# One attention-and-experts kernel: the second block's rows are loaded ahead of the keys and the third's behind them, and TensorE's first pass for the maximum and the turned maximum move ahead of pieces of the keys

## The chip, the cores and the metric

The kernel runs on one NeuronCore of one Trainium2 chip. The metric is the device time of one execution in microseconds (us). The kernel before takes 274.97 us, the median of three runs (274.79 to 275.19). In what follows PE is TensorE (PEld its weight loads), DVE is VectorE, ACT is ScalarE, POOL is GpSimd and SP is SyncE, which here only issues DMAs.

## The reference

1024 tokens of 128 values attend to 6404 keys of 96 values, and then go through a mixture of 8 experts, two of which are used for each token.

```python
def layernorm(x): return (x - mean(x)) / sqrt(var(x) + 1e-5)

def attention(xn, ctx):
    q, k, v = xn @ Wq + bq, ctx @ Wk + bk, ctx @ Wv + bv
    return softmax(q @ k.T / sqrt(128)) @ v

def ffn(xn):
    route = softmax(xn @ Wr + br)
    routed = top-2 of route, scaled to sum 1
    h = relu(xn @ W1[e] + b1[e])
    return sum over e of routed[e] * (h @ W2[e] + b2[e])

x = x + tanh(g_xattn) * attention(layernorm(x), ctx)
x = x + tanh(g_ffn)   * ffn(layernorm(x))
```

## The kernel before, in words

**Tiling.** The 8 tiles of 128 tokens form three blocks of 2, 3 and 3 tiles (`BLOCK_TILES`). The keys form 51 chunks of 128, of which the last holds 4 keys. Loads come in groups of 8 chunks (`NATURAL_GROUP`), transposes in windows of 4 chunks (`WINDOW`, 13 windows, 0 to 12), and the attention of one block goes through 26 units of 2 chunks.

**Precision.** A float32 product is made of three fast products: each operand is split into a rounded part (`_hi`) and the rest (`_lo`). The scores of a chunk are `ctxT_hi*q_hi + ctxT_hi*q_lo + ctxT_lo*q_hi` (L1473 to L1475).

**The softmax's shift.** The maximum of a row is estimated first from the hi parts alone: `score_for_max(s)` on PE makes one *slot*, the scores of one tile of tokens against up to 1024 keys (L1395, two matmuls of 512), and `reduce_max(s)` on DVE reduces it (L999). The first block needs, before its first unit, only round 0: six slots, the two tiles against keys 0 to 1023 (slots 0 and 1, windows 0 and 1), 1024 to 2047 (slots 2 and 3) and 2048 to 3071 (slots 4 and 5). `finish_max(0)` on DVE joins them into `nmax` (L1006), `turn_max(0)` on PE turns `nmax` into a row (L1408), `row_max(0)` on DVE adds it to row 96 of `q_hi` (L1014), and then the product itself subtracts the maximum. Slot s waits until slot s-2 has been reduced, and slot 1 also waits for `q_lo`.

**The start**, the place of this change. There is no scheduler: every engine's instructions stand in the order in which the code writes them, and semaphores tie the engines together.

- SP (L503 to L524) issues the first block's rows of x (`tok`, semaphore `x_in`), the two parts of Wk, group 0 of the keys (8 chunks, 384 KB), all other rows of x (6 tiles, 384 KB, `x_later_in`), groups 1 to 6 of the keys, and then the small constants.
- DVE: `statistics(0, 0)` and the normalized rows of the first block (L1032); then it waits for `x_later_in`, takes `statistics(0, 1)` and `statistics(0, 2)` of the second and third block (L981, L984, L986), makes `q_lo` (L991), the six reductions, `finish_max(0)`, `row_max(0)`, and splits windows 9, 10 and 11 (L1021).
- PE: 10, 4 and 6 warm-up transposes (L1335; the 6 are `WARM_NORM`) around the folding of the weights, the first block's rows turned (`turn_x(0, 0)`, L1368), windows 0 and 1 (`turn_window`, L1359, one transpose for each chunk), the folded q of the block (`make_qk(0)`, L1375), windows 2 and 3, then the six slots with two windows behind slots 1, 3 and window 8 last, the second block's rows, windows 9 and 10, `turn_max(0)`, windows 11 and 12, and then the units: `scores` and, two units later, `values` (L1499 to L1501).
- ACT copies each turned window twice, rounded (`ctxT_hi`, L799) and, for windows 0 to 8, whole (`ctxT_f`, L804); `q_hi` (L814) stands behind the rounded copies of windows 0 and 1. Each unit then takes two exponentials on ACT (L906, L910) and one subtraction on DVE (L1214, `ex_lo`); the scores of unit u wait for `ex_lo` of unit u-2.
- POOL makes `rstd` of each block (L609), the normalized rows of the second and third block (L616), and the `_lo` parts of windows 0 to 8 (L638) and of the keys (L645, L647).

The functions in full:

Of the kernel before, what the change touches and what calls it, by code (L numbers as in the profile page):

```python
# [35 lines left out]
BLOCK_TILES = [2, 3, 3]  # L36
# [3 lines left out]
WINDOW = 4  # L40
# [4 lines left out]
W_RING = 2  # L45
WARM_UP = 10
WARM_FOLD = 4
WARM_NORM = 6
EPS = 1e-5


# [36 lines left out]
def attention_experts(nc, x, ctx, g_xattn, g_ffn, wq, bq, wk, bk, wv, bv, w1, b1, w2, b2, wr, br, out):  # L88
# [83 lines left out]
    with ExitStack() as stack:  # L172
# [3 lines left out]
        def sem(name):  # L176
            return stack.enter_context(nc.semaphore(name))
# [143 lines left out]

        small_in, x_in, w_consts_in = sem("small_in"), sem("x_in"), sem("w_consts_in")
        x_later_in = sem("x_later_in")
        ctx_in = [sem(f"ctx_in{g}") for g in range(NG)]
        w_in = [sem(f"w_in{r}") for r in range(W_SLOTS)]
        out_done = sem("out_done")
# [45 lines left out]
        def tiles(b):  # L372
            return slice(FIRST_TILE[b], FIRST_TILE[b] + BLOCK_TILES[b])
# [130 lines left out]
        def _(sync):  # L504
            sync.dma_start(tok[:, tiles(0), :], xv[:, tiles(0), :]).then_inc(x_in, 16)
            sync.dma_start(wk_sb[0:C, :], wk).then_inc(small_in, 16)
            sync.dma_start(wk_sb[C:CA, :], bk.rearrange("(a h) -> a h", a=1)).then_inc(small_in, 16)
            for g in range(NG):
                js = group_chunks(g)
                whole = min(js[-1] + 1, FULL)  # L510
                sync.dma_start(raw[:, js[0]:whole, :], ctxv[:, js[0]:whole, :]).then_inc(ctx_in[g], 16)
                if g == 0:
                    later = slice(BLOCK_TILES[0], NT)
                    sync.dma_start(tok[:, later, :], xv[:, later, :]).then_inc(x_later_in, 16)
            sync.wait_ge(pad_zeroed, 1)
            sync.dma_start(raw[0:TAIL, FULL, :], ctx[0, FULL * P:NKEY, :]).then_inc(ctx_in[NG - 1], 16)
            sync.dma_start(wv_sb[0:C, 0:HID], wv).then_inc(w_consts_in, 16)
# [72 lines left out]
        def _(pool):  # L590
# [50 lines left out]
            def split_ctx(g):  # L641
                js = group_chunks(g)
                hi = ch[:, js[0]:js[-1] + 1, 0:C]
                pool.wait_ge(ctx_in[g], 16 if js[-1] < FULL else 32)
                nc.gpsimd.tensor_copy(hi, raw[:, js[0]:js[-1] + 1, :]).then_inc(ctx_hi_ready, 1)  # L645
                pool.wait_ge(ctx_hi_ready, g + 1)
                nc.gpsimd.tensor_tensor(cl[:, js[0]:js[-1] + 1, :], raw[:, js[0]:js[-1] + 1, :],  # L647
                                        hi.bitcast(F32), ALU.subtract).then_inc(ctx_lo_ready, 1)
# [321 lines left out]
        def _(dve):  # L970
# [8 lines left out]
            def statistics(which, b):  # L979
                for t in range(BLOCK_TILES[b]):  # L980
                    last = nc.vector.bn_stats(stats[:, which, FIRST_TILE[b] + t, :], tok[:, FIRST_TILE[b] + t, :])  # L981
                step(last)
                for t in range(BLOCK_TILES[b]):
                    last = nc.vector.bn_aggr(mv[:, which, FIRST_TILE[b] + t, :], stats[:, which, FIRST_TILE[b] + t, :])  # L984
                step(last)
                nc.vector.tensor_scalar(veps[:, which, tiles(b)], mv[:, which, tiles(b), 1], EPS, None,  # L986
                                        ALU.add).then_inc(var_ready, 1)
# [14 lines left out]
            def finish_max(r):  # L1002

                ts = tiles(ROUND_BLOCK[r])
                dve.wait_ge(max_reduced, SLOTS_UNTIL[r])
                nc.vector.tensor_reduce(nmax[:, ts], pmax[:, ts, ROUND_AT[r]:ROUND_AT[r] + PLACES[r] + (1 if r == 1 else 0)], AX.X, ALU.max,  # L1006
                                        negate=True).then_inc(nmax_ready, 1)
# [26 lines left out]
            last.then_inc(first_norm, 1)  # L1034
            dve.wait_ge(x_later_in, 16)
            statistics(0, 1)
            statistics(0, 2)
            split_q(0)
            for s in range(SLOTS_UNTIL[0]):
                reduce_max(s)  # L1040
            finish_max(0)
            row_max(0)
            for w in range(TURNED_BY_VECTOR, NW - 1):
                split_window(w)
# [286 lines left out]
        def _(pe):  # L1331
# [15 lines left out]
            def turn_window(w):  # L1347

                js = window_chunks(w)
                pe.wait_ge(ctx_in[js[0] // NATURAL_GROUP], 16 if js[-1] < FULL else 32)  # L1350
                if 4 <= w < TURNED_BY_VECTOR:
                    pe.wait_ge(ctxT_f_ready, w - 3)
                elif w >= TURNED_BY_VECTOR + 2:

                    pe.wait_ge(max_reduced, SLOTS_UNTIL[0] - (NW - 1 - w))
                elif w >= TURNED_BY_VECTOR:
                    pe.wait_ge(ctxT_f_ready, w - 2)
                for k, j in enumerate(js):
                    last = nc.tensor.transpose(window_bank(w)[0:C, k * P:(k + 1) * P], raw[:, j, :], ident[:, :])  # L1359
                last.then_inc(ctx_turned, 1)  # L1360
# [52 lines left out]
            turn_window(0)  # L1413
            turn_window(1)
            make_qk(0)
            for w in range(2, 4):
                turn_window(w)
            for s in range(SLOTS_UNTIL[0]):
                score_for_max(s)
                w = 4 + s  # L1420
                if s % 2 and w < TURNED_BY_VECTOR:
                    turn_window(w - 1)
                    turn_window(w)
            turn_window(TURNED_BY_VECTOR - 1)
            pe.wait_ge(ctxT_f_ready, TURNED_BY_VECTOR - 3)
            turn_x(0, 1, x_home(1))
            for w in range(TURNED_BY_VECTOR, NW - 2):
                turn_window(w)
            turn_max(0)
            for w in range(NW - 2, NW):  # L1430
                turn_window(w)

            def beside_first_block(i):
# [300 lines left out]
```

## Time and profile before

| | us |
|---|---|
| median of 3 runs | 274.97 (274.79 to 275.19) |
| the profiled execution's own time | 274.55 |
| its span in the trace | 272.8 |
| PE busy in the span | 266.0 (98%) |
| DVE, ACT, POOL busy | 210.5, 186.8, 109.3 |
| mean granted TensorE clock | 0.999 of full |

The page lists the share of the span in which each engine had an instruction under way. Its chain of waits is followed back from the last instruction, at each step to what released it. The timeline gives start, duration and the instruction; where a row ends in `xN`, N instructions are merged, and a bracket says how long the engine had been idle and which event ended that. Line numbers are those of the kernel before unless said otherwise.

### The profile page before, as it was taken

To read this page: it belongs to the slowest core of one execution; us is meant where nothing else is said; L and a number is where in the kernel's file an instruction comes from. 1 tells how busy PE (TensorE), PEld (TensorE's weight loads), DVE (VectorE), ACT (ScalarE), POOL (GpSimd) and SP (SyncE) were. 2 spreads that over 40 slices of the span, in tenths; PEclk is the share of its full clock that TensorE was granted. 3 is DMA by queue.
4 is the path that set the end of the run, shared out by engine and by line. 5 is a ranking of instruction groups with operands and counts; after the bars stand their busy time and mean duration, and the time that the engine had idled before them with its cause. 6 is when DMAs were issued, how large, how long until landed. Compare 5 with 4: busy or idle time off the path is not lost.

```text
span 272.8 us, 5070 instructions
## 1 busy us (share of the span) xinstructions
PE 266.0 (98%) x1662; PEld 245.4 (90%) x1662; DVE 210.5 (77%) x406; ACT 186.8 (69%) x338; POOL 109.3 (40%) x144
## 2 busy tenths in 40 slices
PE   7999999999999999999999999999999999999994
PEld 7677989999999999999889999999889998999993
DVE  4889977897486898789637478876688699467696
ACT  2997575445675556556577798888546664999990
POOL 3899993556800030000001553661025444355720
PEclk9999999999999999999999999999999999999999
DMA  6700020000099100000000222435301011313312
GB/s 191 275 2 0 0 82 0 2 1 2 0 248 338 42 0 2 0 1 2 1 0 2 77 77 79 117 126 145 106 15 37 24 32 35 91 58 73 86 53 81
DMA packets 18485, 17.08 MB, mean 63 GB/s; under 512 B 2410, under 2 KB 14940, under 8 KB 18460
## 3 DMA queue, kind: packets, MB, share of 16 engines
q1 hardware_dynamic: 17372, 15.31, 18.7%
q0 software_dynamic: 640, 1.31, 1.7%
q8 instruction: 14, 0.23, 0.3%
q10 hardware_dynamic: 448, 0.14, 0.2%
q14 instruction: 11, 0.09, 0.1%
HBM read 13.34 MB, written 3.42 MB: 61 GB/s over the span
## 4 chain that ended last, share of the span: by engine, by line
PE 87%; DVE 8%; DMA 2%; issue 1%; ACT 1%; SPq 1%; DVEq 0%
PE ps L1473 9%; PE ps L1499 9%; PE ps L1474 9%; PE ps L1500 9%; PE ps L1501 9%; PE ps L1475 9%; PE ps L1395 7%; PE ps L1600 4%; PE ps L1586 3%; DVE pmax L999 2%; DMA tok<-in_x_dram 2%; PE ps L1575 2%; PE ps L1625 2%; PE ps L1627 2%; PE ps L1626 2%; PE ps L1601 2%
## 5 line engine op out<-in xcount | busy, mean ns | idle before, releaser
L906 ACT ACTIVATE ex_hi<-ps 128x768 fp32r<-128x768 f32 (+1 forms) x78 | 56.9, 730 | 55.9 <-PE ps L1475 54.4
L1214 DVE TENSOR_TENSOR ex_lo<-ps,ex_hi 128x768 fp32r<-128x768 f32 (+1 forms) x66 | 58.4, 885 | 23.0 <-ACT ps L910 20.7
L999 DVE TENSOR_REDUCE pmax<-ps 128x1 f32<-128x512 f32 (+2 forms) x74 | 62.4, 874 | 10.3 <-PE ps L1395 9.5
L1499 PE MATMUL ps<-ex_hi,ctx_both 128*97 128x384 f32 (+1 forms) x153 | 49.7, 325 | 0.0
L910 ACT ACTIVATE ps<-ps 128x768 f32<-128x768 f32 (+1 forms) x66 | 49.7, 752 | 0.0
L1474 PE MATMUL ps<-q_lo,ctxT_hi 96*128 96x384 f32 (+1 forms) x153 | 49.0, 321 | 0.0
L1475 PE MATMUL ps<-q_hi,ctxT_lo 96*128 96x384 f32 (+1 forms) x153 | 48.6, 318 | 0.0
L1500 PE MATMUL ps<-ex_hi,ctx_both 128*96 128x384 f32 (+1 forms) x153 | 48.6, 318 | 0.0
L1501 PE MATMUL ps<-ex_lo,ctx_both 128*97 128x384 f32 (+1 forms) x153 | 48.6, 318 | 0.0
L1473 PE MATMUL ps<-q_hi,ctxT_hi 97*128 97x384 f32 (+1 forms) x126 | 42.3, 336 | 0.3 <-DVE ex_lo L1214 0.2
L1395 PE MATMUL ps<-ctxT_hi,q_hi 97*128 97x512 f32 (+1 forms) x104 | 34.3, 400 | 0.7 <-DVE pmax L999 0.4
L609 POOL TENSOR_TENSOR rstd<-veps,minus_half 128x3 f32<-128x3 f32 (+1 forms) x6 | 5.0, 829 | 74.6 <-DVE veps L986 74.4
L1474 PEld LDWEIGHTS ps<-q_lo,ctxT_hi 96*128 96x128 f32 x153 | 29.1, 190 | 0.3
L1475 PEld LDWEIGHTS ps<-q_hi,ctxT_lo 96*128 96x128 f32 x153 | 29.1, 190 | 0.0
L1500 PEld LDWEIGHTS ps<-ex_hi,ctx_both 128*96 128x96 f32 x153 | 24.8, 162 | 3.3
L1499 PEld LDWEIGHTS ps<-ex_hi,ctx_both 128*97 128x97 f32 x153 | 24.8, 162 | 2.8 <-issue 0.7
L1501 PEld LDWEIGHTS ps<-ex_lo,ctx_both 128*97 128x97 f32 x153 | 24.8, 162 | 1.4
L1473 PEld LDWEIGHTS ps<-q_hi,ctxT_hi 97*128 97x128 f32 x126 | 23.7, 188 | 2.5 <-issue 1.1
L1307 DVE TENSOR_TENSOR ex_lo<-ps,ex_hi 128x384 fp32r<-128x384 f32 x32 | 17.7, 554 | 9.3 <-ACT ps L948 8.0
L742 POOL TENSOR_TENSOR shared<-shared 128x128 f32<-128x128 f32 x17 | 8.2, 485 | 31.8 <-ACT shared L937 31.6
L669 POOL TENSOR_TENSOR ex_lo<-shared,ex_hi 128x512 fp32r<-128x512 f32 (+1 forms) x12 | 14.8, 1239 | 13.3 <-PE ps L1501 11.5
L1395 PEld LDWEIGHTS ps<-ctxT_hi,q_hi 97*128 97x128 f32 x104 | 17.4, 189 | 2.5 <-DVE pmax L999 1.2
(227 smaller groups left out, 545.2 us busy)
## 6 DMA issues: line engine op xcount, KB each, us to landing
raw<-in_ctx_dram SPq DMA_DIRECT2D x6, 384.0 KB, 6.1
w_raw<-in_L_ffn_W_dram SPq DMA_DIRECT2D x8, 256.0 KB, 3.9
raw<-in_L_ffn_W_dram SPq DMA_DIRECT2D x8, 256.0 KB, 6.3
raw<-in_L_ffn_b_dram SPq DMA_DIRECT2D x8, 256.0 KB
shared<-routing SPq DMA_DIRECT2D x8, 192.0 KB
x_slots<-shared SPq DMA_DIRECT2D x1, 1088.0 KB, 6.3
y_slots<-shared SPq DMA_DIRECT2D x17, 64.0 KB, 1.5
shared<-in_L_ffn_b_dram SPq DMA_DIRECT2D x1, 512.0 KB, 3.4
```

Source lines behind the costliest of these rows:

```text
L906: nc.scalar.activation(ex_pair(ex_hi, u % P_RING, js, n), scores, ACT.Exp)
L910: nc.scalar.activation(whole, scores, ACT.Exp).then_inc(ex_ready, 1)
L999: nc.vector.tensor_reduce(pmax[:, FIRST_TILE[ROUND_BLOCK[r]] + t, place:place + 1], max_home(s)[:, 0:w], AX.X, ALU.max).then_inc(max_reduc ...
L1214: nc.vector.tensor_tensor(ex_pair(ex_lo, u % P_RING, js, n), whole, ex_pair(ex_hi, u % P_RING, js, n).bitcast(F32), ALU.subtract).then_inc ...
L1307: nc.vector.tensor_tensor(hid(ex_lo, u), bank_of_hidden(u)[:, 0:SPAN], hid(ex_hi, u).bitcast(F32), ALU.subtract).then_inc(h_lo_ready, 1)
L1395: last = nc.tensor.matmul(max_home(s)[:, at:at + n], q_hi[:, ft * P:(ft + 1) * P], ctxT_hi[0:CA, key + at:key + at + n], start=True, stop= ...
L1473: nc.tensor.matmul(dst, ctxT_hi[0:CA, keys], q, start=True, stop=False)
L1474: nc.tensor.matmul(dst, ctxT_hi[0:C, keys], q_lo[:, span(b)], start=False, stop=False)
L1475: last = nc.tensor.matmul(dst, ctxT_lo[0:C, keys], q_hi[0:C, span(b)], start=False, stop=True)
L1499: nc.tensor.matmul(dst[0:CA, :], ch[:, j, :], hi, start=(j == first), stop=False)
L1500: nc.tensor.matmul(dst[0:C, :], cl[:, j, :], hi, start=False, stop=False)
L1501: last = nc.tensor.matmul(dst[0:CA, :], ch[:, j, :], lo, start=False, stop=(j == final))
```

## The change

On SP, the second block's rows (3 tiles, 192 KB, `x_later_in`) are issued ahead of the keys; group 0 of the keys is issued as two halves of 4 chunks with a semaphore each (`ctx_first_in` for window 0); the third block's rows (192 KB, `x_last_in`) are issued behind the last group. On DVE, `statistics(0, 2)` moves from ahead of `q_lo` to between `finish_max(0)` and `row_max(0)`, behind a wait for `x_last_in`. On PE, `WARM_NORM` falls from 6 to 2, windows 2 and 3 move from ahead of slot 0 to behind it, and windows 9 and 10 move behind `turn_max(0)`. POOL's `split_ctx(0)` waits for both halves. No computation is added or taken away but the four warm-up transposes; there is one DMA more in group 0 and one more for x.

```diff
-WARM_NORM = 6
+WARM_NORM = 2
...
+            sync.dma_start(tok[:, tiles(1), :], xv[:, tiles(1), :]).then_inc(x_later_in, 16)
             for g in range(NG):
                 js = group_chunks(g)
                 whole = min(js[-1] + 1, FULL)
+                if g == 0:
+                    sync.dma_start(raw[:, 0:WINDOW, :], ctxv[:, 0:WINDOW, :]).then_inc(ctx_first_in, 16)
+                    js = js[WINDOW:]
                 sync.dma_start(raw[:, js[0]:whole, :], ctxv[:, js[0]:whole, :]).then_inc(ctx_in[g], 16)
-                if g == 0:
-                    later = slice(BLOCK_TILES[0], NT)
-                    sync.dma_start(tok[:, later, :], xv[:, later, :]).then_inc(x_later_in, 16)
+            sync.dma_start(tok[:, tiles(2), :], xv[:, tiles(2), :]).then_inc(x_last_in, 16)
...
             dve.wait_ge(x_later_in, 16)
             statistics(0, 1)
-            statistics(0, 2)
             split_q(0)
             for s in range(SLOTS_UNTIL[0]):
                 reduce_max(s)
             finish_max(0)
+
+            dve.wait_ge(x_last_in, 16)
+            statistics(0, 2)
             row_max(0)
...
             def turn_window(w):
                 js = window_chunks(w)
-                pe.wait_ge(ctx_in[js[0] // NATURAL_GROUP], 16 if js[-1] < FULL else 32)
+                if w == 0:
+                    pe.wait_ge(ctx_first_in, 16)
+                else:
+                    pe.wait_ge(ctx_in[js[0] // NATURAL_GROUP], 16 if js[-1] < FULL else 32)
...
             make_qk(0)
-            for w in range(2, 4):
-                turn_window(w)
+
             for s in range(SLOTS_UNTIL[0]):
                 score_for_max(s)
-                w = 4 + s
-                if s % 2 and w < TURNED_BY_VECTOR:
+                w = 3 if s == 0 else 4 + s
+                if (s == 0 or s % 2) and w < TURNED_BY_VECTOR:
                     turn_window(w - 1)
                     turn_window(w)
             turn_window(TURNED_BY_VECTOR - 1)
             pe.wait_ge(ctxT_f_ready, TURNED_BY_VECTOR - 3)
             turn_x(0, 1, x_home(1))
-            for w in range(TURNED_BY_VECTOR, NW - 2):
-                turn_window(w)
             turn_max(0)
-            for w in range(NW - 2, NW):
+            for w in range(TURNED_BY_VECTOR, NW):
                 turn_window(w)
```

How the instructions stand, first on PE at the start. L1335 is a warm-up transpose, L1368 turns rows of x, L1359 turns a chunk of keys, L1375 makes q, L1395 is half a slot. Before:

```order
L1335 MATMUL ps<-ident 128x128 x6
L1368 MATMUL ps<-ident,norm 128x128 x2
L1359 MATMUL ps<-ident,raw 96x128 x8
L1375 MATMUL ps<-xT,mq_sb 97x256
L1359 MATMUL ps<-ident,raw 96x128 x8
L1395 MATMUL ps<-ctxT_hi,q_hi 128x512 x4
L1359 MATMUL ps<-ident,raw 96x128 x8
L1395 MATMUL ps<-ctxT_hi,q_hi 128x512 x4
```

And in the changed kernel, where the same lines are L1345, L1381, L1372, L1388 and L1408:

```order
L1345 MATMUL ps<-ident 128x128 x2
L1381 MATMUL ps<-ident,norm 128x128 x2
L1372 MATMUL ps<-ident,raw 96x128 x8
L1388 MATMUL ps<-xT,mq_sb 97x256
L1408 MATMUL ps<-ctxT_hi,q_hi 128x512 x2
L1372 MATMUL ps<-ident,raw 96x128 x8
L1408 MATMUL ps<-ctxT_hi,q_hi 128x512 x2
L1372 MATMUL ps<-ident,raw 96x128 x8
L1408 MATMUL ps<-ctxT_hi,q_hi 128x512 x4
```

Slot 0 now stands ahead of windows 2 and 3, and slot 1 between them and windows 4 and 5.

PE at the end of round 0, from the last two slots to the first unit. L1408 turns the maximum and L1473 is the first matmul of unit 0. Before:

```order
L1395 MATMUL ps<-ctxT_hi,q_hi 128x512 x4
L1359 MATMUL ps<-ident,raw 96x128 x4
L1368 MATMUL ps<-ident,norm 128x128 x3
L1359 MATMUL ps<-ident,raw 96x128 x8
L1408 MATMUL ps<-ident,nmax 1x128 x2
L1359 MATMUL ps<-ident,raw 96x128 x7
L1473 MATMUL ps<-q_hi,ctxT_hi 128x256
```

In the changed kernel (L1421 turns the maximum, L1483 begins unit 0):

```order
L1408 MATMUL ps<-ctxT_hi,q_hi 128x512 x4
L1372 MATMUL ps<-ident,raw 96x128 x4
L1381 MATMUL ps<-ident,norm 128x128 x3
L1421 MATMUL ps<-ident,nmax 1x128 x2
L1372 MATMUL ps<-ident,raw 96x128 x15
L1483 MATMUL ps<-q_hi,ctxT_hi 128x256
```

Eight transposes went from ahead of the turned maximum to behind it, where there are now 15 instead of 7.

DVE, from the first block's normalized rows to the split windows. Before:

```order
L1032 TENSOR_SCALAR norm<-tok,mv,rstd 128x128 x2
L981 BN_STATS stats<-tok 128x6 x3
L984 BN_AGGR mv<-stats 128x2 x3
L986 TENSOR_SCALAR veps<-mv 128x3
L981 BN_STATS stats<-tok 128x6 x3
L984 BN_AGGR mv<-stats 128x2 x3
L986 TENSOR_SCALAR veps<-mv 128x3
L991 SCALAR_TENSOR_TENSOR q_lo<-ps,bias_col,q_hi 96x256
L999 TENSOR_REDUCE pmax<-ps 128x1 x6
L1006 TENSOR_REDUCE nmax<-pmax 128x2
L1014 TENSOR_TENSOR q_hi<-ps,q_hi 1x256
L1021 TENSOR_TENSOR ctxT_lo<-ps,ctxT_hi 96x512 x3
```

In the changed kernel:

```order
L1040 TENSOR_SCALAR norm<-tok,mv,rstd 128x128 x2
L989 BN_STATS stats<-tok 128x6 x3
L992 BN_AGGR mv<-stats 128x2 x3
L994 TENSOR_SCALAR veps<-mv 128x3
L999 SCALAR_TENSOR_TENSOR q_lo<-ps,bias_col,q_hi 96x256
L1007 TENSOR_REDUCE pmax<-ps 128x1 x6
L1014 TENSOR_REDUCE nmax<-pmax 128x2
L989 BN_STATS stats<-tok 128x6 x3
L992 BN_AGGR mv<-stats 128x2 x3
L994 TENSOR_SCALAR veps<-mv 128x3
L1022 TENSOR_TENSOR q_hi<-ps,q_hi 1x256
L1029 TENSOR_TENSOR ctxT_lo<-ps,ctxT_hi 96x512 x3
```

The third block's seven instructions of statistics left the place ahead of `q_lo` and stand between `nmax` and the row of the maximum.

## Rows read from the trace of the kernel before

**Rows 1.** The page: granted TensorE clock in 40 slices; the chain's shares by engine.

```profile
PEclk9999999999999999999999999999999999999999
...
PE 87%; DVE 8%; DMA 2%; issue 1%; ACT 1%; SPq 1%; DVEq 0%
```

**Rows 2.** Chain of waits, first 25 us: start us, us, what.

```profile
7.37 0.69 DVE stats L981 x3
...
8.60 0.59 DVE stats L981 x3
...
10.11 6.80 DVE pmax L999 x6
16.93 0.17 DVE nmax L1006
...
17.15 0.60 PE ps L1408 x4
...
19.41 0.60 ACT ex_hi L906
```

**Rows 3.** DMA issues in windows 2.03:2.4, 2.4:2.9, 2.9:3.4: KB each, us to landing.

```profile
raw<-in_ctx_dram SPq DMA_DIRECT2D x1, 384.0 KB, 4.3
...
tok<-in_x_dram SPq DMA_DIRECT2D x1, 384.0 KB, 4.9
...
raw<-in_ctx_dram SPq DMA_DIRECT2D x1, 384.0 KB, 5.4
```

**Rows 4.** Timeline of SP's queue: the issues of those three.

```profile
2.06 0.35 SPq L511 DMA_DIRECT2D raw<-in_ctx_dram  x1
2.45 0.43 SPq L514 DMA_DIRECT2D tok<-in_x_dram  x1
2.93 3.46 SPq L511 DMA_DIRECT2D raw<-in_ctx_dram  x6
```

**Rows 5.** Timeline of PE: start us, us, instruction, [idle before <-releaser].

```profile
5.79 0.86 PE L1335 MATMUL ps<-ident 128*128 128x128 f32 x6
...
6.71 1.04 PE L1359 MATMUL ps<-ident,raw 128*96 128x128 f32 x8
...
9.17 0.71 PE L1395 MATMUL ps<-ctxT_hi,q_hi 97*128 97x512 f32 x2
10.17 0.73 PE L1395 MATMUL ps<-ctxT_hi,q_hi 97*128 97x512 f32 x2 [0.29 <-DVE q_lo L991]
10.74 1.04 PE L1359 MATMUL ps<-ident,raw 128*96 128x128 f32 x8
11.53 0.71 PE L1395 MATMUL ps<-ctxT_hi,q_hi 97*128 97x512 f32 x2
...
15.27 0.60 PE L1359 MATMUL ps<-ident,raw 128*96 128x128 f32 x4
...
16.04 1.04 PE L1359 MATMUL ps<-ident,raw 128*96 128x128 f32 x8
...
17.68 0.97 PE L1359 MATMUL ps<-ident,raw 128*96 128x128 f32 x7
18.41 0.36 PE L1473 MATMUL ps<-q_hi,ctxT_hi 97*128 97x256 f32 x1
```

**Rows 6.** Timeline of ACT.

```profile
7.34 1.07 ACT L799 CAST ctxT_hi<-ps 97x512 fp32r<-97x512 f32 x2
8.30 0.49 ACT L814 ACTIVATE q_hi<-ps,bias_col 97x256 fp32r<-97x256 f32 x1
...
17.24 2.08 ACT L799 CAST ctxT_hi<-ps 96x512 fp32r<-96x512 f32 x4
```

**Rows 7.** Timeline of DVE.

```profile
5.23 0.60 DVE L1032 TENSOR_SCALAR norm<-tok,mv,rstd 128x128 f32<-128x128 f32 x2 [0.92 <-POOL rstd L609]
...
17.78 0.43 DVE L1014 TENSOR_TENSOR q_hi<-ps,q_hi 1x256 fp32r<-1x256 f32 x1 [0.69 <-PE ps L1408]
```

**Rows 8.** Timeline of POOL: the lo parts of windows 0 to 3.

```profile
12.06 4.97 POOL L638 TENSOR_TENSOR ctxT_lo<-w_raw,ctxT_hi 96x512 fp32r<-96x512 f32 x4
```

More of the change, by code:

```diff
@@ L323, in attention_experts @@
         x_later_in = sem("x_later_in")
+        ctx_first_in = sem("ctx_first_in")
+        x_last_in = sem("x_last_in")
         ctx_in = [sem(f"ctx_in{g}") for g in range(NG)]
@@ L643, in split_ctx @@
                 hi = ch[:, js[0]:js[-1] + 1, 0:C]
+                if g == 0:
+                    pool.wait_ge(ctx_first_in, 16)
                 pool.wait_ge(ctx_in[g], 16 if js[-1] < FULL else 32)
```

## The prediction

> **What bounds the kernel now.** I read the page first. The chain that ended last lies for 87% on PE and for 8% on DVE [rows 1], so nearly everything behind the start is PE's own work. The change leaves that work as it is. It can only move the time at which the first unit starts, so I read the first 25 us of the chain of waits. There the limit is DVE: it waits for the later rows of x, takes two sets of statistics from 7.37, and then runs six reductions back to back from 10.11 to 16.93, 1.14 us each; nmax follows, PE turns it at 17.15, and the first exponential starts at 19.41 [rows 2]. Of everything in the change I therefore ask what it does to three times: when slot 0 reaches DVE, when nmax is taken (N, 16.93 now), and when the first exponential starts (X, 19.41 now). From X on the same instructions follow in the same order, so a shift of X should be a shift of the end.
>
> **The loads.** Group 0 of the keys is issued at 2.06, the rows of x at 2.45, group 1 at 2.93 [rows 4], and they land 4.3, 4.9 and 5.4 us later [rows 3]: at 6.36, 7.35 and 8.33. That is 384 KB every 0.98 us, in order of issue, so I take bytes in order as the rule: 192 KB cost 0.49 us. The new order puts the second block's rows at 6.36 - 0.49 = 5.87, window 0's half at 6.36, window 1's at 6.85 and group 1 at 7.84. So window 0's keys come when all of group 0 came before, and what follows is half a microsecond earlier until the third block's rows, which come last.
>
> The Trainium skill (DMA: Bandwidth & Descriptors, Anatomy of one DMA) gives a DMA about 2.0 us plus its bytes at 436 GB/s, for the path through GpSimd. By that page's figures, as an estimate, 192 KB issued at 2.45 land at 4.9, and the keys would not be waited for at all. The trace disagrees for this queue: 384 KB took 4.3 to 5.4 us here [rows 3], since each DMA stands behind the ones ahead of it. I go by the trace.
>
> **Slot 0.** Before, windows 0 and 1 start on PE at 6.71, behind the warm-up and the turned rows [rows 5]. ACT begins to copy window 0 at 7.34 (0.63 later), copies two windows in 0.96 and makes q_hi from 8.30 to 8.79 [rows 6]. Slot 0 could then have started near 8.85, but two other things held the reductions: windows 2 and 3 stood ahead of it on PE, to 9.17 [rows 5], and q_lo stood behind the statistics on DVE, so that slot 0, ready at 9.17 + 0.71 = 9.88, was reduced from 10.11 [rows 2, 5]. After the change the normalized rows are ready at 5.83 as before [rows 7]. Four warm-up transposes less (0.86 for 6, overlapping [rows 5], so about 0.5) let PE turn them at once, which would allow window 0 from about 6.2. It then waits for its keys to 6.36, and window 1 for its half to 6.85. Window 1 sets the rest: its copy begins 0.63 later, q_hi another 0.48 later and takes 0.49, and 0.06 passes to PE. Slot 0 starts at t = 6.85 + 0.03 + 0.63 + 0.48 + 0.49 + 0.06 = **8.54**. Its scores reach DVE at t + 0.76 = 9.30. The second block's statistics (1.23 from set to set [rows 2]) are over by 7.2, and q_lo (0.4) fits between q_hi and slot 0. So the first reduction starts 0.81 earlier than now.
>
> **A new gap.** Half of that is given back. A slot holds PE for 0.57 (10.17 to 10.74), two windows for 0.79 (10.74 to 11.53) [rows 5]. The new order has windows 2 and 3 behind slot 0 and windows 4 and 5 behind slot 1, so slot 2 starts at t + 2 x (0.57 + 0.79) = t + 2.72 and its scores are there at t + 3.48, while DVE has finished two reductions at t + 0.76 + 2.27 = t + 3.03. DVE idles 0.45. Slots 3 to 5 stay ahead of DVE. N = t + 0.76 + 6.82 + 0.45 = t + 8.03 = **16.57**, 0.36 earlier than 16.93.
>
> **Behind nmax.** Before, windows 9 and 10 ran from 16.04, in the time in which PE had to wait for nmax anyway [rows 5]; they cost nothing there. Now they come after it. PE turns the maximum 0.22 after N, starts the windows 0.53 later (17.15 to 17.68), and 7 transposes take 0.73 to the first unit at 18.41 [rows 2, 5], 0.104 each. Fifteen take 1.56, which is 0.83 more. The first unit starts at 16.57 + 0.22 + 0.53 + 1.56 = **18.88** in place of 18.41, and X follows 1.00 later as now, at 19.88.
>
> Is another engine later than that? ACT: window 9's copy can begin only at 17.32 + 0.63 = 17.95. Three more starts at 0.48 and the last copy (0.49) end at 19.88, at the same moment; before, ACT had begun these four at 17.24 and was through at 19.32 [rows 6]. DVE: third-block statistics from 16.74 take 1.23, and row_max, now behind them, runs 17.97 to 18.40 instead of 17.78 to 18.21 [rows 7]. PE reaches the first unit 0.48 after that, so the statistics cost nothing as long as the 15 transposes cover them. If windows 9 and 10 were still ahead, the row would be the limit, at about 18.45. What is queued behind the new wait for the third block's rows is row_max and then the split windows; those rows land near 13, over 3 us ahead. POOL: its split of windows 0 to 3 ends at 17.03 [rows 8], and the second block's normalized rows, which stand ahead of it, come no later than now. SP's two more issues and POOL's longer wait for group 0 lie behind landed loads with microseconds to spare. I cost these at nothing.
>
> **Sum.** -0.36 (N earlier) + 0.83 (windows behind it) = +0.47, rounded to **+0.5** because two engines meet at X. The profiled execution took 274.55, of which the span is 272.8, so its twin would take 275.05; the median of before is 0.42 above that execution, so I put the changed kernel's median at **275.5**. What a measurement of this kernel can tell from no change is about 0.2%, 0.55 us, and the sum lies just inside.
>
> **The bounds.** The unknown is the landing of the two halves with shorter runs. Below, PE is held only by the turned rows: t = 8.35 and X +0.3. Above, if DMAs cost by number and not by bytes, window 1's half lands third, at 8.33: t = 10.0 and X +1.9. I stay near the lower one, since the rows show bytes in order at a steady pace.
>
> **Rivals.**
>
> *The keys come late (slower).* If halves with half the run length move more slowly, window 1's half lands after 7.1 instead of 6.85. For it: the load stands behind 192 KB of x that PE does not need. Against: the steady 0.98 us steps. From a delay of 0.25 on, the sum is +0.7; with half of the upper bound it is +1.2, 276.2. Chance 0.18.
>
> *The clock falls (slower).* All 40 slices show the granted clock at 0.9 or more of full, the 2.4 GHz level [rows 1]. After slot 5 PE would now turn window 8 and the second block's rows, then idle from 15.7 to 16.8 where before it turned windows, then turn 15 chunks. If the clock fell to 1.2 GHz there, those 15 transposes and unit 0 (1.56 + 1.00) would take up to twice as long: +2.6 on top, 278.1. The Trainium skill (TensorE: Matmul & The Clock Gate, Part 4: PE-mode transpose) says that transposes do not count as busy for the clock as matmuls do, and by that rule this stretch, with fewer warm-ups ahead, is a risk. The trace disagrees so far: from 15.27 to 18.41 PE did little but transposes already, and the clock held. Chance 0.05.
>
> *The shift is absorbed (no change).* DVE paces units 2 to 4, so a late X might be made up there. Against it: DVE's work there starts from X's own result, and nothing in it is taken out. It would give 275.0 to 275.2. Chance 0.17.
>
> *The end is earlier (faster).* N would have to come 1.4 us earlier, to pay 0.83 for the windows and 0.55 more: slot 0 at t = 7.5 at the latest. That needs q_hi by 7.4, when window 0's keys have landed for 1 us and two copies stand ahead on ACT. I see no way but a gain in later units that the trace does not announce. 274.3. Chance 0.09.
>
> **Numbers.** The forecast itself has 0.51, for X from +0.3 to +0.75; six tenths of that fall within 0.2%. Same: 0.6 x 0.51 + 0.15 of the absorbed case = 0.46. Slower: 0.4 x 0.51 + 0.18 + 0.05 + the other 0.02 of it = 0.45. Faster: 0.09. The range goes from 274.7 (some absorption, and run-to-run spread of 0.2) to 276.3 (the late keys with half the bound), and leaves out the faster case and the clock.
>
> **What would show it.** Right: slot 0 near 8.5; a gap of about 0.4 on DVE between the second and third reduction; nmax near 16.6; PE idle about a microsecond ahead of the turned maximum; 15 transposes behind it and the first unit near 18.9; row_max done before that; X near 19.9 and no difference later. Wrong: window 0 or 1 waiting for its keys past 7.0, nmax later than 16.9 or earlier than 16.2, the first unit waiting for row_max, a granted clock below full between 16 and 20, or a gain or loss behind 25 us.

## The result, and the profile after

The changed kernel takes 275.81 us, the median of seven runs (275.78 to 276.18), against 274.97 (274.61 to 275.20) for the kernel before, timed beside it: slower by 0.84 us, ratio 1.0034 with a 95% interval of 1.0022 to 1.0046. The forecast was 275.5 in a range of 274.7 to 276.3, with nearly even chances for "the same" and "slower". In the runs below two executions lie more than 1.5% above the fastest of their kernel, at 279.35 with the addition on POOL and at 279.21 for the kernel before in the third set; the ratios leave them out, and without them those two medians are 275.94 and 275.20.

| us | before | worked out | after |
|---|---|---|---|
| profiled execution (its span) | 274.55 (272.8) | 275.05 | 275.78 (274.0) |
| slot 0 starts on PE | 9.17 | 8.54 | 8.42 |
| first reduction starts | 10.03 (10.11 in [rows 2]) | 9.30 | 9.17 |
| nmax is taken (N) | 16.93 | 16.57 | 16.49 |
| first unit starts on PE | 18.41 | 18.88 | 19.57 |
| first exponential starts (X) | 19.41 | 19.88 | 20.59 |

Up to N everything came as worked out, to within 0.13. From X on, the shift of 1.18 is carried to the end, where it is 1.23; in the chains of waits the same instructions stand 1.15 later near 70 us and 1.22 near 200. The time was lost between N and the first unit, and more of it than forecast.

First the loads. These are the DMA issues in four short stretches, with KB each and us to landing, for the issues at 2.06, 2.46, 2.93 and 3.4:

```profile
tok<-in_x_dram SPq DMA_DIRECT2D x1, 192.0 KB, 3.4
...
raw<-in_ctx_dram SPq DMA_DIRECT2D x1, 192.0 KB, 3.6
...
raw<-in_ctx_dram SPq DMA_DIRECT2D x2, 192.0 KB, 3.6
...
raw<-in_ctx_dram SPq DMA_DIRECT2D x1, 384.0 KB, 4.2
```

They land at 5.5, 6.1, 6.5 and 7.6, each 0.2 to 0.4 earlier than worked out from [rows 3]. PE's timeline, which answers to [rows 5]:

```profile
8.42 0.71 PE L1408 MATMUL ps<-ctxT_hi,q_hi 97*128 97x512 f32 x2 [0.75 <-ACT q_hi L822]
8.96 1.04 PE L1372 MATMUL ps<-ident,raw 128*96 128x128 f32 x8
9.76 0.71 PE L1408 MATMUL ps<-ctxT_hi,q_hi 97*128 97x512 f32 x2
10.31 1.04 PE L1372 MATMUL ps<-ident,raw 128*96 128x128 f32 x8
11.10 1.42 PE L1408 MATMUL ps<-ctxT_hi,q_hi 97*128 97x512 f32 x4
...
16.70 0.60 PE L1421 MATMUL ps<-ident,nmax 128*1 128x128 f32 x4 [0.96 <-DVE nmax L1014]
17.23 1.84 PE L1372 MATMUL ps<-ident,raw 128*96 128x128 f32 x15
19.57 0.39 PE L1483 MATMUL ps<-q_hi,ctxT_hi 97*128 97x256 f32 x1 [0.49 <-DVE q_hi L1022]
```

Ahead of slot 0 PE waits for q_hi, and the trace shows no wait for keys before it. Slot 2 starts 2.68 after slot 0 (2.72 worked out), and PE idles 0.96 before it turns the maximum. All that was expected, but for the keys, which the prediction had as the limit. The last row was not: the first unit waits 0.49 for the row of the maximum, which I had ready 0.48 ahead of PE. DVE's timeline shows what came late:

```profile
6.77 0.71 DVE L994 TENSOR_SCALAR veps<-mv 128x3 f32<-128x3 f32 x1
8.30 0.48 DVE L999 SCALAR_TENSOR_TENSOR q_lo<-ps,bias_col,q_hi 96x256 fp32r<-96x256 f32 x1 [0.82 <-ACT q_hi L822]
9.17 7.29 DVE L1007 TENSOR_REDUCE pmax<-ps 128x1 f32<-128x1024 f32 x6 [0.38 <-PE ps L1408]
16.49 0.16 DVE L1014 TENSOR_REDUCE nmax<-pmax 128x2 f32<-128x6 f32 x1
16.57 0.67 DVE L989 BATCH_NORM_STATS2 stats<-tok 128x6 f32<-128x128 f32 x3
17.27 0.31 DVE L992 BATCH_NORM_AGGREGATE mv<-stats 128x2 f32<-128x6 f32 x3
17.62 1.43 DVE L994 TENSOR_SCALAR veps<-mv 128x3 f32<-128x3 f32 x1
19.08 0.43 DVE L1022 TENSOR_TENSOR q_hi<-ps,q_hi 1x256 fp32r<-1x256 f32 x1
```

The six reductions take 7.29 where they took 6.87 in the same view, which is the gap that was forecast. Then look at `veps`. It is the last of the seven instructions of the third block's statistics: it adds eps to 128x3 values. It took 1.43 us. In the trace of the kernel before, the additions of the second and third block took this long:

```profile
8.43 0.17 DVE L986 TENSOR_SCALAR veps<-mv 128x3 f32<-128x3 f32 x1
...
9.56 0.17 DVE L986 TENSOR_SCALAR veps<-mv 128x3 f32<-128x3 f32 x1
```

Its inputs were there in both kernels, since it follows on DVE what makes them. And there is no idle time in front of it; the trace shows the loss as a long instruction. POOL's timeline in the changed kernel has the other half:

```profile
5.86 1.59 POOL L630 MEMSET ctxT_hi<- 1x1796 f32 x1 [0.70 <-DVE norm L1040]
...
16.43 0.83 POOL L653 CAST ctx_both<-raw 128x768 fp32r<-128x768 f32 x1
17.34 1.69 POOL L655 TENSOR_TENSOR ctx_both<-raw,ctx_both 128x768 fp32r<-128x768 f32 x1
```

POOL's subtraction runs from 17.34 to 19.03, and `veps` ends at 19.05. The second block's `veps`, at 6.77, shows it a second time: it took 0.71 and ended at 7.48, in the last part of POOL's memset (5.86 to 7.45). There it costs nothing, since q_hi, for which DVE waits next, comes at 8.30. Around it nothing is slowed: `stats` takes 0.67 beside POOL's cast and `mv` 0.31 beside its subtraction, as in the second block (and 0.67 to 0.68 and 0.31 to 0.32 in the kernel before), and the reductions, which read PSUM, last 1.21 to 1.23 beside POOL's work, no longer than the one at 44.8 us of the kernel before, where POOL is idle (1.23). The Trainium skill (SBUF — State Buffer, Who interferes with whom) has a rule for this: of VectorE and GpSimd, whichever starts first holds a shared pair of SBUF ports for its whole instruction and the other blocks; `tensor_scalar` can need that pair, `tensor_reduce` never does. The trace agrees, 1.43 against 0.17 for the one and no change for the other; that the pair of ports is the reason is the page's account, and the trace shows only that the one instruction lasts until the other's end.

So this was my theory of the extra loss, the **shut-out**: `veps` cannot run while POOL's subtraction does, and row_max stands behind it. Without it the row would have been ready at 17.62 + 0.17 + 0.03 + 0.43 = 18.25, PE would have set the first unit with the end of its 15 transposes, near 18.83, and the loss would have been the forecast 0.4. (ACT's copies of windows 9 to 12, 17.91 to 19.84 here, would have let X start at that same time.) Its rivals: that the late first unit belongs to the windows behind the maximum alone; and that the start (loads, warm-ups, the clock) decides and differs from execution to execution.

### The profile page after: what moved, and what is told of

Read it like the earlier page. It is cut to its first block, busy times and chain, and to the rows that moved or that the text cites. A ratio compares the mean times of both kernels' runs of the same rounds, so it can differ in the third digit from the quotient of the medians.

```text
span 274.0 us, 5065 instructions
## 1 busy us (share of the span) xinstructions
PE 265.6 (97%) x1658; PEld 245.0 (89%) x1658; DVE 212.6 (78%) x406; ACT 186.9 (68%) x338; POOL 109.5 (40%) x144
## 4 chain that ended last, share of the span: by engine, by line
PE 80%; DVE 7%; DMA 5%; issue 3%; ACT 2%; POOL 2%; ACTq 0%; DVEq 0%; POOLq 0%
PE ps L1483 9%; PE ps L1509 9%; PE ps L1484 9%; PE ps L1510 9%; PE ps L1511 9%; PE ps L1485 9%; PE ps L1408 8%; DMA w_raw<-y_slots,slot 4%; PE ps L1610 4%; PE ps L1596 2%; DVE pmax L1007 2%; PE ps L1585 2%; PE ps L1586 1%; PE ps L1587 1%; PE ps L1611 1%
## 5 line engine op out<-in xcount | busy, mean ns | idle before, releaser
L1483 PE MATMUL ps<-q_hi,ctxT_hi 97*128 97x384 f32 (+1 forms) x126 | 42.3, 336 | 0.8 <-DVE q_hi L1022 0.5
L1408 PE MATMUL ps<-ctxT_hi,q_hi 97*128 97x512 f32 (+1 forms) x104 | 34.2, 399 | 1.1 <-ACT q_hi L822 0.8
L1483 PEld LDWEIGHTS ps<-q_hi,ctxT_hi 97*128 97x128 f32 x126 | 23.7, 188 | 3.2 <-issue 0.8
L1408 PEld LDWEIGHTS ps<-ctxT_hi,q_hi 97*128 97x128 f32 x104 | 17.4, 189 | 2.9 <-DVE pmax L1007 1.2
```

The costliest lines, as they stand in the source:

```text
L1408: last = nc.tensor.matmul(max_home(s)[:, at:at + n], q_hi[:, ft * P:(ft + 1) * P], ctxT_hi[0:CA, key + at:key + at + n], start=True, stop= ...
L1483: nc.tensor.matmul(dst, ctxT_hi[0:CA, keys], q, start=True, stop=False)
```

## The experiments

Each was timed in alternation with the kernel before on the same chip, in three sets; the kernel before had a median of 275.14 in the first, 275.17 in the second and 275.27 in the third. It does not take one time but spreads from 274.4 to 276.5, so differences of a few tenths are read from medians of about 12 runs, and mechanisms from the traces. Edits are against the changed kernel unless said otherwise. Nothing is left out of the computation in any of them.

### The changed kernel again (set 2)

> The changed kernel itself, beside the others of this set. In the trace of the first set its first unit waits for an instruction that ends when GpSimd's subtraction ends (19.05), so what happens before N, up to about 17.5, cannot move it. Theory A: its times lie close together, 275.8 to 276.0, on any chip, and the first unit starts at 19.5 to 19.6 again. Rival: its times spread like those of the kernel with eps on GpSimd (275.2 to 276.4), and the narrow spread seen so far was chance.

Measured: 275.85 (275.78 to 277.36, 12 runs), ratio 1.0030 [1.0015, 1.0045]. Ten of the twelve lie between 275.78 and 276.11, and no execution of the changed kernel is below 275.78. DVE's timeline:

```profile
17.36 0.31 DVE L992 BATCH_NORM_AGGREGATE mv<-stats 128x2 f32<-128x6 f32 x3
17.71 1.38 DVE L994 TENSOR_SCALAR veps<-mv 128x3 f32<-128x3 f32 x1
```

The shut-out repeats: it started 0.09 later and ended 0.04 later, at 19.09, with POOL's subtraction at 19.06. That also explains the floor under the times. The end of POOL's work does not depend on when N comes: in the nine profiles with this kernel's loads and POOL's order of work the subtraction starts at 17.33 to 17.39, with N anywhere from 16.34 to 17.48. So an execution with an early N gains nothing from it.

### The eps addition moved to POOL (set 1)

```diff
             def statistics(which, b):
...
+                if which == 0 and b == 2:
+                    last.then_inc(var_ready, 1)
+                    return
                 nc.vector.tensor_scalar(veps[:, which, tiles(b)], mv[:, which, tiles(b), 1], EPS, None,
                                         ALU.add).then_inc(var_ready, 1)
...
             def inverse_deviation(k):
...
                 pool.wait_ge(var_ready, k + 1)
+                if k == 2:
+                    step(nc.gpsimd.tensor_scalar(veps[:, which, tiles(b)], mv[:, which, tiles(b), 1], EPS, None, ALU.add))
```

> The changed kernel, with the one DVE instruction that took 1.43 us there (the 128x3 addition of eps, from 17.62 to 19.05, otherwise 0.17) made on GpSimd instead. Theory A (DVE is shut out of a shared way into SBUF until GpSimd's subtraction, 17.34 to 19.03, is over, and this alone carried the row of the maximum past the 15 transposes): row_max runs from about 17.65, the first unit starts behind the transposes near 18.85 in place of 19.57, the first exponential near 19.87, and the time is 0.7 us under the changed kernel, 275.1 to 275.4. Theory B (the 15 transposes and the late maximum set the start, the long addition was covered): the first unit stays near 19.5 and the time near 275.8.

Measured: 275.96 (275.22 to 279.35, 12 runs), ratio 1.0028 [1.0016, 1.0041]. DVE, then PE:

```profile
16.88 0.16 DVE L1019 TENSOR_REDUCE nmax<-pmax 128x2 f32<-128x6 f32 x1
...
18.00 0.43 DVE L1027 TENSOR_TENSOR q_hi<-ps,q_hi 1x256 fp32r<-1x256 f32 x1
```

```profile
17.62 1.84 PE L1377 MATMUL ps<-ident,raw 128*96 128x128 f32 x15
19.22 0.36 PE L1488 MATMUL ps<-q_hi,ctxT_hi 97*128 97x256 f32 x1
```

The step went as the theory has it: the row is ready at 18.43, 0.8 ahead of PE, and the first unit waits for nothing. X is 20.23, at which ACT's copies of the windows end too. The time did not: the median is no lower. N came at 16.88 in this profile, 0.39 later than in the changed kernel's, and now that is paid in full (19.22 = 16.88 + 2.34). Without the shut-out the 15 transposes set the end and N's spread is back; the lowest run, 275.22, is 0.56 under the changed kernel's lowest. The expected fall of the median was a miss.

### Windows 9 and 10 back ahead of the maximum (set 1)

```diff
+            for w in range(TURNED_BY_VECTOR, NW - 2):
+                turn_window(w)
             turn_max(0)
-            for w in range(TURNED_BY_VECTOR, NW):
+            for w in range(NW - 2, NW):
                 turn_window(w)
```

> The changed kernel with windows 9 and 10 back ahead of the turned maximum. Theory A (the row of the maximum, late by DVE's long addition, is what the first unit waits for): row_max still ends near 19.5, the first unit stays near 19.57, the time near 275.8, although PE is through with its transposes 0.8 us earlier. Theory B (the transposes behind the maximum are the cost): the first unit moves up by 0.8, to 18.75, and the time falls to 275.0.

Measured: 275.88 (275.78 to 276.93, 12 runs), ratio 1.0030 [1.0014, 1.0046]. DVE, then PE:

```profile
17.83 1.21 DVE L994 TENSOR_SCALAR veps<-mv 128x3 f32<-128x3 f32 x1
```

```profile
17.44 0.97 PE L1372 MATMUL ps<-ident,raw 128*96 128x128 f32 x7
19.55 0.39 PE L1485 MATMUL ps<-q_hi,ctxT_hi 97*128 97x256 f32 x1 [1.15 <-DVE q_hi L1022]
```

and POOL:

```profile
17.33 1.68 POOL L655 TENSOR_TENSOR ctx_both<-raw,ctx_both 128x768 fp32r<-128x768 f32 x1
```

PE has eight transposes less to do behind the maximum and is through by 18.2, and then it waits 1.15 for the row. The first unit starts at 19.55 in place of 19.57, and the time stays, as expected of the shut-out. The windows alone are not the cause: with the shut-out in place they cost nothing.

### Both (set 1)

The two edits above together.

> The changed kernel with both edits: eps added on GpSimd, windows 9 and 10 ahead of the turned maximum. Theory A: the maximum is known at 16.5, row_max ends at 18.1 and PE is through at 18.0, so the first unit starts near 18.15 and the first exponential near 19.2, 0.2 us before the kernel before's 19.41: 274.6 to 274.9. Theory B (each edit alone has its own share and they add without a wait in between): no more than the better of the two alone.

Measured: 274.86 (274.55 to 275.72, 12 runs), ratio 0.9997 [0.9985, 1.0010]. PE's timeline:

```profile
16.76 0.60 PE L1426 MATMUL ps<-ident,nmax 128*1 128x128 f32 x4
17.29 0.97 PE L1377 MATMUL ps<-ident,raw 128*96 128x128 f32 x7
18.15 0.39 PE L1490 MATMUL ps<-q_hi,ctxT_hi 97*128 97x256 f32 x1
```

Time and first unit are as expected. Each edit alone gives no lower median and both together give 1.0 us: two limits stand side by side, the transposes (first unit at N + 2.34) and the shut-out (first unit near 19.57), and the later of them counts.

### The addition as an instruction with two inputs (set 1, one execution)

```diff
-                nc.vector.tensor_scalar(veps[:, which, tiles(b)], mv[:, which, tiles(b), 1], EPS, None,
-                                        ALU.add).then_inc(var_ready, 1)
+                var = mv[:, which, tiles(b), 1]
+                if which == 0 and b == 2:
+                    nc.vector.scalar_tensor_tensor(out=veps[:, which, tiles(b)], in0=var, scalar=EPS, in1=var,
+                                                   op0=ALU.add, op1=ALU.max).then_inc(var_ready, 1)
+                    return
+                nc.vector.tensor_scalar(veps[:, which, tiles(b)], var, EPS, None, ALU.add).then_inc(var_ready, 1)
```

> The changed kernel, with the addition of eps left on DVE but as an instruction with two tensor inputs in SBUF, max(var + eps, var), which cannot use the form that reads one tensor through two ports. If only that fast one-input form is shut out by GpSimd, the addition takes 0.2 us and the first unit starts near 18.85. If an instruction with two SBUF inputs is shut out as well while GpSimd reads SBUF, it takes 1.4 us again and the first unit stays near 19.57.

Measured: 276.06, one execution. DVE, then POOL:

```profile
18.60 0.49 DVE L996 SCALAR_TENSOR_TENSOR veps<-mv 128x3 f32<-128x3 f32 x1
```

```profile
17.39 1.69 POOL L655 TENSOR_TENSOR ctx_both<-raw,ctx_both 128x768 fp32r<-128x768 f32 x1
```

The start was slow in this execution (slot 0 at 9.39, N at 17.48), so the instruction came late into POOL's, but it too ended with it: 19.09 and 19.08. No run shows what this form takes by itself, so how much of the 0.49 is waiting is not shown; that two inputs do not free it is what one execution suggests. The start was so late here that the transposes set the first unit (19.82 = N + 2.34).

### POOL's wait placed ahead of its split (set 3)

On top of the windows' return, the addition stays on DVE, and POOL's `inverse_deviation(2)`, which waits for that addition, moves ahead of its split of the natural keys:

```diff
+            inverse_deviation(2)
             for g in range(0, 2):
                 split_ctx(g)
-            inverse_deviation(2)
```

> The changed kernel with windows 9 and 10 ahead of the turned maximum (as in e2), and on GpSimd the third block's rstd moved ahead of the split of key groups 0 and 1. DVE's statistics are untouched, eps stays on DVE; but GpSimd now waits for them with nothing under way instead of running its subtraction from 17.34 to 19.03. Theory A (DVE's addition is shut out only while GpSimd has an instruction under way): the addition takes 0.2 us, row_max ends near 18.2, the first unit starts near 18.25 in place of 19.55, and the time falls from e2's 275.88 to that of e3, 274.6 to 275.0. Rival (the addition is slow at this place for a reason of DVE's own): it takes over 1 us again and the time stays at 275.9.

Measured: 275.03 (274.47 to 275.63, 11 runs), ratio 0.9991 [0.9975, 1.0008]. DVE, then POOL:

```profile
17.58 0.17 DVE L994 TENSOR_SCALAR veps<-mv 128x3 f32<-128x3 f32 x1
17.78 0.43 DVE L1022 TENSOR_TENSOR q_hi<-ps,q_hi 1x256 fp32r<-1x256 f32 x1
```

```profile
17.83 0.89 POOL L615 TENSOR_TENSOR rstd<-veps,minus_half 128x3 f32<-128x3 f32 x1 [1.31 <-DVE veps L994]
```

PE's first unit:

```profile
18.27 0.39 PE L1485 MATMUL ps<-q_hi,ctxT_hi 97*128 97x256 f32 x1
```

This is the run that settles the cause. The instruction, its engine and its place on DVE are those of the run with windows 9 and 10 back, with 1.21 there and 0.17 here; the only difference in the code is where POOL's wait stands, so that POOL is idle at that moment. The first unit starts at 18.27 (18.25 expected). Against its own set's kernel before it stands at -0.17 (275.03 to 275.20), the run with the windows back at +0.74 (275.88 to 275.14).

### The other half: windows 9 and 10 moved in the kernel before (set 3)

```diff
-            for w in range(TURNED_BY_VECTOR, NW - 2):
-                turn_window(w)
             turn_max(0)
-            for w in range(NW - 2, NW):
+            for w in range(TURNED_BY_VECTOR, NW):
                 turn_window(w)
```

> The kernel before with one edit: windows 9 and 10 behind the turned maximum. The prediction's term by itself: eight transposes of 0.104 us more between the maximum and the first unit, +0.83, time 275.8 to 276.0. If PE had cover there (row_max or ACT later than PE anyway), under +0.3.

Measured: 276.19 (275.73 to 277.47, 12 runs), ratio 1.0042 [1.0025, 1.0060]. PE's timeline:

```profile
17.32 0.60 PE L1408 MATMUL ps<-ident,nmax 128*1 128x128 f32 x4 [0.95 <-DVE nmax L1006]
17.85 1.84 PE L1359 MATMUL ps<-ident,raw 128*96 128x128 f32 x15
19.45 0.36 PE L1471 MATMUL ps<-q_hi,ctxT_hi 97*128 97x256 f32 x1
```

The price of this move by itself: the first unit starts at N + 2.34, where it was N + 1.48 [rows 2, 5], so 0.86. The forecast had 0.83: this term was right. The medians lie 0.99 apart (276.19 and 275.20), the median 0.19 above the range expected of it; the four lowest of the 12 times are 275.73 to 275.80.

### The statistics alone moved in the kernel before (set 3)

```diff
             statistics(0, 1)
-            statistics(0, 2)
...
             finish_max(0)
+            statistics(0, 2)
             row_max(0)
```

> The kernel before with one edit: the third block's statistics between the maximum and its row. nmax is 0.1 to 0.2 earlier (near 16.8). The addition of eps comes up near 17.75, when GpSimd goes from its copy (16.98 to 17.79) to its subtraction (17.88 to 19.58). Theory A: it either gets in between, then row_max ends near 18.4 and the time is 275.0 to 275.3, or it is shut out to 19.58, then the first unit starts near 20.1 and the time is 276.6 to 276.8; executions lie at one of the two. Theory B (no shutting out): always 275.0 to 275.3.

Measured: 277.41 (276.48 to 277.87, 6 runs), ratio 1.0070 [1.0044, 1.0096]. DVE, then PE:

```profile
17.49 0.16 DVE L1006 TENSOR_REDUCE nmax<-pmax 128x2 f32<-128x6 f32 x1
...
18.62 0.92 DVE L986 TENSOR_SCALAR veps<-mv 128x3 f32<-128x3 f32 x1
```

```profile
20.05 0.39 PE L1473 MATMUL ps<-q_hi,ctxT_hi 97*128 97x256 f32 x1 [0.85 <-DVE q_hi L1014]
```

The shut-out appears in the kernel before as soon as the statistics move, with the old loads and the old windows. No execution lies at the 275.0 to 275.3 of an addition that got in between. The size was a miss: 2.2 over the kernel before (277.41 to 275.20); only the two lowest, 276.48 and 276.56, lie near the 276.6 that was expected. In the profile X, at 21.07, is 1.66 later than in the profile of before, and N was late as well (17.49). Some 1.4 us more came in later: the exponentials are 1.66 behind those of before at 141 us and 1.86 at 259 us, and the rest came in behind that. Every other profile has its time 255.1 to 255.5 behind X, and this one 256.6. I did not find out why.

### Windows 2 and 3 back ahead of slot 0 (set 2)

```diff
+            for w in range(2, 4):
+                turn_window(w)
             for s in range(SLOTS_UNTIL[0]):
                 score_for_max(s)
-                w = 3 if s == 0 else 4 + s
-                if (s == 0 or s % 2) and w < TURNED_BY_VECTOR:
+                w = 4 + s
+                if s % 2 and w < TURNED_BY_VECTOR:
```

> The changed kernel with windows 2 and 3 back ahead of slot 0. PE waits 0.75 there for q_hi anyway, and their keys have landed by 7.6, so slot 0 should start within 0.1 of now and the gap of 0.45 on DVE ahead of slot 2 should be gone: nmax near 16.05. Theory A then makes it a matter of who is first: the addition of eps comes up near 17.2, between GpSimd's copy (to 17.26) and its subtraction (17.34 to 19.03). If it gets in first, row_max ends near 17.8, the first unit starts behind the transposes near 18.4 and the time is 274.6 to 274.9; if not, the first unit stays at 19.57 and the time at 275.8 in spite of the earlier maximum. Theory B (no shutting out): always 0.45 less than now, 275.4.

Measured: 275.84 (274.79 to 275.98, 11 runs), ratio 1.0021 [1.0009, 1.0033]. PE at windows 2 and 3, then DVE:

```profile
8.37 1.08 PE L1372 MATMUL ps<-ident,raw 128*96 128x128 f32 x8 [0.24 <-DMA raw<-in_ctx_dram]
```

```profile
18.00 1.09 DVE L994 TENSOR_SCALAR veps<-mv 128x3 f32<-128x3 f32 x1
```

The expectation was a miss at the start: windows 2 and 3 did not fit into PE's wait, since in this execution the first two windows took 1.28 in place of 1.05 and group 1 landed only at 8.3. Slot 0 starts at 9.21 and N is 16.87, 0.38 later than in the changed kernel and not 0.45 earlier, and yet the first unit starts at 19.60, only 0.03 later: the shut-out sets it. `veps` started later and lost less, 1.09, to the same end at 19.09. Ten of the eleven runs lie between 275.77 and 275.98, and one at 274.79. That one fits an addition that got in ahead of POOL's subtraction, but it left no trace.

### All three undone, with the new loads kept (set 2)

Windows 2 and 3, windows 9 and 10 back, and the addition on POOL.

> The changed kernel's loads and warm-up, with windows 2 and 3 ahead of slot 0, windows 9 and 10 ahead of the turned maximum, and eps of the third block added on GpSimd. nmax near 16.05, row_max done near 17.65, PE through at 17.55. ACT's copies of windows 9 to 12 then set the start: first exponential near 18.95 in place of 19.41, time 274.3 to 274.6, under both kernels. If theory A or the gap on DVE were wrong, it would be no better than the kernel with only two of the three edits (274.86).

Measured: 274.87 (274.23 to 276.41, 12 runs), ratio 0.9988 [0.9972, 1.0004]. DVE's timeline:

```profile
16.34 0.16 DVE L1019 TENSOR_REDUCE nmax<-pmax 128x2 f32<-128x6 f32 x1
...
17.47 0.43 DVE L1027 TENSOR_TENSOR q_hi<-ps,q_hi 1x256 fp32r<-1x256 f32 x1
```

Its profile has the earliest X of all, 18.98, and the lowest profiled time, 274.40, inside the expected range. Its median is above that range, and it does not differ from that of before, nor from that with slot 0 early (274.86). The new order of loads is worth at most a few tenths, and I cannot tell them from none.

### Six warm-ups again, and the keys first (sets 2 and 3)

The first is the addition on POOL with `WARM_NORM = 6`. The second is the kernel above with the second block's rows issued behind the two halves of group 0.

> The changed kernel with eps added on GpSimd and all 6 warm-up transposes. Without DVE's long addition nothing hides a late slot 0. Theory C (with 2 warm-ups PE sometimes still turns the first rows and keys at 0.21 us each instead of 0.104, and slot 0 starts up to 0.8 late): the four transposes cost 0.3 to 0.4 when all is well, but the spread shrinks to under 0.6 us and the median falls to 275.5 or less, against 275.96 with 2 warm-ups. Theory D (the spread comes from the landing of the loads): the spread stays over 1 us and the median rises by 0.3 to about 276.2.

Measured: 276.37 (275.45 to 276.93, 8 runs), ratio 1.0036 [1.0020, 1.0053]. The times spread over 1.5 us, where those with 2 warm-ups spread over 1.2 (275.22 to 276.39), so the missing warm-ups are not where the spread comes from.

> As e6, but the two halves of key group 0 are issued ahead of the second block's rows. The rows are needed for DVE's statistics by 7.3 and for q_lo not at all; they should land near 6.9. If the landing of the keys is what makes slot 0 late in many executions, it starts at 8.3 to 8.5 in this one and the median falls by 0.2 to 0.4 under e6's 274.87; if group 1 (windows 2 and 3, lands last of the four either way) or the clock sets it, the median stays at 274.8 to 274.9.

Measured: 275.49 (274.62 to 275.91, 12 runs), ratio 1.0000 [0.9983, 1.0016]. PE's timeline:

```profile
9.15 1.08 PE L1378 MATMUL ps<-ident,raw 128*96 128x128 f32 x8 [0.98 <-DMA raw<-in_ctx_dram]
```

A miss. The two halves landed at 5.1 and 5.6, but in this execution group 1 landed only at 9.1, 5.7 after its issue, and PE waited 0.98 for it. In the changed kernel it landed at 7.6.

## Why the prediction was right in its range, and wrong in a step

- **Loads, slot 0, the gap, N.** Right in the numbers: 8.42 for 8.54, a gap of 0.42 in the reductions for 0.45, N 16.49 for 16.57. The steps in order of issue held (0.6 and 0.5 for 192 KB, 1.1 for 384), but all landed 0.2 to 0.4 earlier. So it was not window 1's half that "sets the rest": slot 0 was held by the turned rows, the case of the lower bound (8.35). And the gap does not lie between the second and the third reduction alone. The slots start 1.34 apart (8.42, 9.76, 11.10) and a reduction holds DVE for 1.13, so DVE idles 0.2 ahead of the second and 0.2 ahead of the third, which the prediction overlooked; the sum is the same.
- **Windows behind nmax.** Right: +0.83 forecast, +0.86 when done alone. Nothing hides it, and ACT meets PE at X as worked out: in the run with the windows alone its copies end at 20.46 and X is 20.45.
- **The statistics behind nmax.** This is the step that failed: "third-block statistics from 16.74 take 1.23, and row_max, now behind them, runs 17.97 to 18.40", and "the statistics cost nothing as long as the 15 transposes cover them". They took 2.48 (16.57 to 19.05), and row_max ran 19.08 to 19.51. The price of 1.23 came from a place at which POOL was idle or within 0.05 of the end of an instruction, and in the new place POOL has one of 1.69 us under way. The trace of the kernel before had the evidence, in POOL's timeline right behind [rows 8]; I read it only for what POOL has to deliver, and gave the term no bound above:

```profile
16.98 0.81 POOL L645 CAST ctx_both<-raw 128x768 fp32r<-128x768 f32 x1
17.88 1.70 POOL L647 TENSOR_TENSOR ctx_both<-raw,ctx_both 128x768 fp32r<-128x768 f32 x1
```

- **Size.** 19.57 - 18.83 = 0.74 on the first unit is the shut-out's share beyond the transposes, and the rest of the 1.16 is the forecast 0.42 to 0.47. The profiled execution came out 0.73 above its own sum (275.78 for 275.05), and the median only 0.31 above the forecast, because of the next point. That the measured time came so near is luck to this extent: the sum lacked a loss of 0.7, and more than half of that was made up by an offset of 0.4 which the sum had and the changed kernel has not.
- **The base.** The prediction put the changed kernel as far above its profiled execution as the median of before stands above its own, 0.42. That does not hold: 275.81 is 0.03 above 275.78. With the floor set by POOL the times gather at one value, where those of before spread.
- **The clock, late keys, absorption.** None of them: the granted clock is 1.00 in every stretch from 16 to 20, the keys were early, and units 2 to 4 made up nothing of the shift (1.18 at X, 1.17 at 30 us).

Settled: the cause of the loss is two limits side by side, the 15 transposes (shown with and without them, and alone in the kernel before) and the shut-out (shown by an idle POOL, by moving the addition, and by moving the statistics alone). Open: why the start differs by up to 1 us between executions (the last section shows what the late ones have in common, not why), what the statistics' run lost at the end, and whether a combination beats the kernel before. The three best (both edits, all three, POOL's wait first) have intervals that include 1.

## What to carry to other kernels

Before a small instruction of VectorE moves onto a critical stretch, look at what GpSimd runs at that moment, not only at what it has to deliver: here an addition to 128x3 values cost the rest of a 1.69 us subtraction. Such a loss stands in the trace as a long duration, not as a wait, so compare the duration of the same instruction at two places. And where undoing one part of a change gives nothing, undo two before you clear either; a second limit just behind the first hides it.

## What the hardware showed that I had not expected

- A `tensor_scalar` of 128x3 float32 values on DVE takes 0.17 us by itself and 1.43, 1.38, 1.21, 1.09 and 0.92 when it starts under POOL's subtraction, each time ending 0.02 to 0.03 us behind it. Under a memset, which reads nothing, it took 0.71. The price followed the rest of POOL's instruction, not the work of DVE's own.
- PE's transposes of the start follow each other at 0.21 us and later ones at 0.104 to 0.109, at a recorded granted clock of 1.00 in both. In ten of the fourteen profiles the change has come by 5.9 us. It came near 6.2 with windows 2 and 3 back, 6.7 with the keys first, 7.4 with the two inputs and 7.5 in the statistics' run. The last two have their late starts from it: slot 0 at 9.39 for 8.42, and at 9.84 for 9.17. The latest has all six warm-ups, so they do not prevent it; there they took 1.52 in place of 0.86 [rows 5]:

```profile
5.80 1.52 PE L1335 MATMUL ps<-ident 128*128 128x128 f32 x6
7.11 0.64 PE L1368 MATMUL ps<-ident,norm 128*128 128x128 f32 x2
```

- The same load can land 1.5 us apart: group 1 of the keys at 7.6 in the changed kernel and at 9.1 in the run with the keys first, behind the same 576 KB in another order.
